# Cross attentions: where ScalarE copies the turned rows in its step

## The chip, the cores and the metric

The kernel runs on one core of a Trainium2 chip. The metric is the device time in microseconds (us) of one execution of the whole program. The program holds an attention and a feed-forward block four times over; the change touches two of the four attentions.

## The reference

`x` has 32 sequences of 128 rows of 128 numbers, and `ctx_768` holds, for each sequence, 128 rows of 96 numbers. The program is a chain, and each line is added to `x`:

```
x = x + L0_xattn(layernorm(x), ctx)         # cross attention, 16 heads of 8, with biases and wo  <- changed
x = x + L0_ffn(layernorm(x))                # 8 experts, top 1
x = x + L1_xattn(layernorm(x), ctx)         # one head
x = x + L1_ffn(layernorm(x))                # 15 experts, top 3
x = x + L2_xattn(layernorm(x), ctx, mask)   # cross attention, 16 heads of 8, masked rows         <- changed
x = x + L2_ffn(layernorm(x))                # causal self attention, 16 heads of 8, then 8 experts
x = x + L3_xattn(layernorm(x), ctx)         # 8 heads of 64
x = x + L3_ffn(layernorm(x))                # 8 experts with capacity
```

The two changed attentions compute, per sequence, with `h` the normalised rows:

```
q = h @ Wq (+ bq);  k, v = ctx @ Wk (+ bk), ctx @ Wv (+ bv)
out = softmax(q k^T / sqrt(8)) v   per head;  out @ wo + bo in L0, out itself in L2
```

## The kernel before

`attention16(p, before, kind)` builds three of the attentions: `kind` is `cross` for L0, `masked` for L2 and `self` (`causal`) for the attention inside L2_ffn. An item is one sequence, 32 in all. Each engine runs a loop of steps, `for item in unrolled(...)`, and in step t it works on several items at different depths: `item(lag)` is item t - lag. In the two cross attentions F is 1, L is 2 and O is 6. Every engine carries out its own list strictly in the order in which it is written; between the engines there are only semaphores. So the order of the calls within a step is a hand-written schedule.

For one item the path is this (engines in brackets, lag behind the name):

- [VectorE] `stats`, `aggregate` (0) and `norm` (1) make `h`; GpSimd makes the reciprocal root between them (`rsqrt`).
- [TensorE] `pe_hT` (F) turns `h` into bank `FR` of PSUM; [ScalarE] `a_hT` (F) copies these turned rows to `hT` in SBUF; [TensorE] `pe_qkv` (F) multiplies `hT` and the context by the weights, L376 and L377, into `FR` again.
- [VectorE] `v_qkv` (F) takes q and k out (L553 in the cross, L556 and L558 in the masked attention) and v (L566 or L569). `pe_turn` (L) waits for that, turns q and k, and `v_kx` and `a_qT` copy them.
- [VectorE, GpSimd] `high` and `g_low` (F + 1) split q and k into parts of fewer bits; [TensorE] `pe_stack_k` and `pe_stack_q` (L + 1) stack them, and [ScalarE] `a_qS` (four copies, L842) and `a_kS` (L834) copy the stacks to SBUF.
- [TensorE] `pe_scores` (L), in two halves, gives the scores of which `v_max` (L667) takes the maxima of each half; `pe_scoresT` (L + 2), in two halves, gives the turned scores, and [ScalarE] `a_exp` (L865) takes their exponentials, half 0 and half 1, each 128x1024.
- [TensorE] `pe_values` (L + 3) multiplies the exponentials by v and by ones, [VectorE] `v_heads` (L + 3) takes the reciprocal and multiplies (L675, L679), [TensorE] `pe_out` (O) writes the projection (or a turn back) into the bank of the k stack, and `v_residual` adds it to `X`.

The waits of the copy that the change moves, and of the two instructions that it is moved past, are these:

```
def a_hT:  wait s_qkv (an item RING earlier);  wait s_hps (it.n + 1);  copy hT <- FR;  inc s_hT
def a_kS:  wait s_st (two halves of an older item);  wait s_tk (it.n + 1);  copy kS <- TP[1];  inc s_kS
def a_exp: wait s_av (an older item);  wait s_st (2 * it.n + half + 1);  P <- exp(ST_ps);  inc s_exp
```

Who waits for them: `pe_qkv` for `s_hT`; `pe_out` (and, a step later, the turned scores and the next k stack) for `s_kS`; `pe_scoresT` of half 1 for the first half's `s_exp`, and `pe_values` for both halves.

Of the kernel before, what the change touches and what calls it, by code (L numbers as in the profile page):

```python
# [54 lines left out]
def due(value):  # L55

    return not isinstance(value, int) or value > 0
# [7 lines left out]
def unrolled(last):  # L65

    def tick(t):
        return lambda lag: Item((t - lag) // RING, (t - lag) % RING) if 0 <= t - lag < B else None
    for t in range(B + last):
        yield tick(t)  # L70


def build(nc, a, out):
    ctx = ExitStack()
    with ctx:
# [226 lines left out]
        def attention16(p, before, kind):  # L302
# [7 lines left out]
            F = 2 if causal else 1  # L310
            L = 4 if causal else 2
# [337 lines left out]
            def high(e, it):  # L649
                if due(it.n - RING + 1):  # L650
                    e.wait_ge(s_tq, at(s_tq, it.n - RING + 1))
                e.wait_ge(s_qkf, at(s_qkf, (2 if causal else 1) * (it.n + 1)))
                src = qk[:, it.s % 2].rearrange("p a h d -> p (a h) d").unsqueeze(2).broadcast_to([T, 2 * H16, 3, DH])
                dst = parts[:, it.s, :, :, 0:3, :].rearrange("p a h c d -> p (a h) c d")
                (e.copy if causal else e.tensor_copy)(dst, src).then_inc(s_hi, 1)  # L655
# [164 lines left out]
            def a_kx(e, it):  # L820
                e.wait_ge(s_turn, at(s_turn, it.n + 1))
                for j in range(4):
                    m = e.activation(kx[:, it.s % 2, j, :], FR[:, T:2 * T], ACT.Copy, scale=jmask[:, j:j + 1])
                m.then_inc(s_kx, 1)

            def a_qT(e, it):
                e.wait_ge(s_kx, at(s_kx, it.n + 1))
                e.copy(qT[:, it.s, :], FR[:, 0:T]).then_inc(s_qT, 1)

            def a_kS(e, it):  # L830
                if due(2 * (it.n - 1)):
                    e.wait_ge(s_st, at(s_st, 2 * (it.n - 1)))
                e.wait_ge(s_tk, at(s_tk, it.n + 1))
                e.copy(kS[:, it.s % 2].rearrange("p g t -> p (g t)"), TP[1]).then_inc(s_kS, 1)  # L834

            def a_qS(e, it):
                if due(2 * (it.n - 1)):
                    e.wait_ge(s_st, at(s_st, 2 * (it.n - 1)))
                e.wait_ge(s_tq, at(s_tq, it.n + 1))
                for j in range(4):  # L840
                    r = slice(32 * j, 32 * j + 32)
                    m = e.copy(qS[r, it.s % 2, :, j, :], TP[0][r, :].rearrange("p (g t) -> p g t", g=4))  # L842
                m.then_inc(s_qS, 1)

            def a_hT(e, it):
                if due(it.n - RING + 1):
                    e.wait_ge(s_qkv, at(s_qkv, it.n - RING + 1))
                e.wait_ge(s_hps, at(s_hps, it.n + 1))
                if causal:
                    e.activation(hT[:, it.s, :], FR[:, 0:T], ACT.Identity, scale=w[p + "ln"][:, 0:1]).then_inc(s_hT, 1)  # L850
                else:
                    e.copy(hT[:, it.s, :], FR[:, 0:T]).then_inc(s_hT, 1)

            def a_gate(e, it):
                if due(it.n):
                    e.wait_ge(s_gt, at(s_gt, it.n))
                e.wait_ge(s_gate, at(s_gate, it.n + 1))
                e.activation(eg[:, it.s % 3, :], TP[1][:, 0:T], ACT.Tanh, bias=half_bgate[:, 0:1], scale=0.5)\
                 .then_inc(s_eg, 1)

            def a_exp(e, it, half):
                if due(it.n - 1):
                    e.wait_ge(s_av, at(s_av, it.n - 1))
                e.wait_ge(s_st, at(s_st, 2 * it.n + half + 1))
                e.activation(P[:, it.s % 2, 8 * half:8 * half + 8, :].rearrange("p h t -> p (h t)"),  # L865
                             ST_ps[:, :, :].rearrange("p j n -> p (j n)"), ACT.Exp,
                             scale=float(DH) ** -0.5).then_inc(s_exp, 1)

            def scalar(e):
                before(e)  # L870
                e.wait_ge(s_pad, at(s_pad, n_pad))
                if causal:
                    for item in unrolled(G):
                        if it := item(L):
                            a_kx(e, it)
                            a_qT(e, it)
                        if it := item(L + 1):
                            a_kS(e, it)
                        if it := item(F + 2):
                            high(e, it)  # L880
                        if it := item(L + 2):
                            a_exp(e, it, 0)
                        if it := item(L + 1):
                            a_qS(e, it)
                        if it := item(F):
                            a_hT(e, it)
                        if it := item(G):
                            a_gate(e, it)
                        if it := item(L + 2):
                            a_exp(e, it, 1)  # L890
                else:
                    for item in unrolled(L + 3):
                        if it := item(L):
                            a_qT(e, it)
                        if it := item(L + 1):
                            a_qS(e, it)
                            a_kS(e, it)
                        if it := item(L + 2):
                            a_exp(e, it, 0)
                        if it := item(F):  # L900
                            a_hT(e, it)
                        if it := item(L + 2):
                            a_exp(e, it, 1)
            totals(stats=B, rstd=B, h=B, bn=B, ve=B, hps=B, hT=B, qkv=B, qkf=B * (2 if causal else 1), v=B,
# [7 lines left out]
            else:  # L912
                totals(**{f"ctx{i}": 16 * GROUPS for i in range(RING)})
            return dict(ahead=ahead, sync=sync, tensor=tensor, vector=vector, gpsimd=pool, scalar=scalar,
                        done=(s_done, reached["done"]))

# [1697 lines left out]
```

## Time and profile before

| | us |
|---|---|
| median of 3 runs | 2060.94 |
| lowest and highest | 2058.76 and 2067.56 |
| the profiled execution | 2070.73 |
| its span (first to last instruction) | 2068.9 |
| L0 cross attention, full steps | about 54 to 269 |
| L2 masked attention, full steps | about 873 to 1092 |

Over the span TensorE's matmuls are busy 78%, its weight loads 62%, VectorE 65%, ScalarE 46% and GpSimd 38%. In the rows below a line such as "L852" is line 852 of the kernel; PE is TensorE, PEld its weight loads, DVE is VectorE, ACT is ScalarE and POOL is GpSimd. What stands in square brackets behind a row of the timeline is the time for which the engine had been idle before it, and what ended that.

### The profile page before, as it was taken

How to read it: one execution, taken by the hardware profiler on the slowest of the kernel's cores; microseconds unless marked ns; L12 is line 12 of the kernel's file. 1: busy time of each engine (PE TensorE's matmuls, PEld its weight loads, DVE VectorE, ACT ScalarE, POOL GpSimd, SP SyncE). 2: the span in 40 equal slices, each digit the busy share in tenths (PEclk: the TensorE clock that was granted, in tenths of full speed). 3: DMA queues.
4: the chain of work that ended last, by engine and by line, in shares of the span. 5: the costliest groups of instructions: out<-in, count | busy, mean ns of one | idle time of the engine just before them, and what ended most of it. 6: DMA issues, size and time to landing. Idle time of an engine off the chain costs nothing. (4 is left out here: it accounts for less than half of the span.)

```text
span 2068.9 us, 42298 instructions
## 1 busy us (share of the span) xinstructions
PE 1615.1 (78%) x14686; PEld 1274.7 (62%) x14686; DVE 1346.9 (65%) x4040; ACT 944.5 (46%) x1817; POOL 776.0 (38%) x1156
## 2 busy tenths in 40 slices
PE   5888863877799989788885899998549799999440
PEld 3666552876677778455553566665448699997330
DVE  4777754238787777577774788886547477774632
ACT  2666630533343334366663677777124344443010
POOL 2222226345300000111213677774454544442435
PEclk9999985887799999699997799999659799999565
DMA  6132301841000000000000000000037000000043
GB/s 181 49 129 69 107 6 37 253 142 40 25 1 2 0 1 1 6 9 7 8 5 1 1 2 2 2 2 2 16 116 231 21 14 14 15 14 3 21 135 89
DMA packets 60416, 91.88 MB, mean 44 GB/s; under 512 B 11587, under 2 KB 49492, under 8 KB 59668
## 3 DMA queue, kind: packets, MB, share of 16 engines
q1 hardware_dynamic: 54068, 76.67, 12.0%
q0 software_dynamic: 6144, 12.60, 2.0%
q8 instruction: 115, 1.88, 0.4%
q14 instruction: 89, 0.73, 0.1%
HBM read 72.71 MB, written 35.39 MB: 52 GB/s over the span
## 5 line engine op out<-in xcount | busy, mean ns | idle before, releaser
L667 DVE TENSOR_REDUCE parts<-PS 128x8 fp32r<-128x1024 f32 x192 | 234.6, 1222 | 153.8 <-PE PS L424 153.6
L865 ACT ACTIVATE P<-PS 128x1024 f32<-128x1024 f32 x192 | 197.0, 1026 | 154.9 <-PE PS L439 154.7
L842 ACT CAST qS<-PS 32x512 fp32r<-32x512 f32 x384 | 220.9, 575 | 9.1 <-PE PS L391 5.7
L272 POOL TENSOR_TENSOR ve<-mv,eps_t 128x1 f32<-128x1 f32 x160 | 33.3, 208 | 444.9 <-DVE mv L268 444.9
L1636 DVE SCALAR_TENSOR_TENSOR X<-PS,wt,X 128x128 f32 (+1 forms) x480 | 134.7, 343 | 48.9 <-PE PS L1479 41.4
L1479 PEld LDWEIGHTS PS<-w_f_w,P 128*128 128x128 f32 x1024 | 131.1, 194 | 39.3 <-issue 27.2
L1768 ACT ACTIVATE P<-PS,w_f_b 128x512 f32<-128x512 f32 x128 | 88.0, 687 | 143.7 <-PE PS L1460 142.3
L1479 PE MATMUL PS<-w_f_w,P 128*128 128x128 f32 x1024 | 143.1, 284 | 13.0 <-DVE X L1636 11.2
L439 PE MATMUL PS<-qS,kS 128*128 128x512 f32 x384 | 148.9, 442 | 1.0 <-ACT P L865 1.0
L762 POOL TENSOR_TENSOR rrs<-rsq,neg_half 128x20 f32<-128x20 f32 x32 | 114.3, 3571 | 74.5 <-DVE rsq L597 74.5
L391 PE MATMUL PS<-ident_r,parts 128*128 128x128 f32 x768 | 122.0, 292 | 23.1 <-issue 22.4
L391 PEld LDWEIGHTS PS<-ident_r,parts 128*128 128x128 f32 x768 | 103.5, 201 | 37.6 <-issue 35.9
L2277 POOL DMA_INDIRECT hs<-hD,idx x96 | 93.6, 975 | 67.0 <-issue 23.8
L456 PE MATMUL PS<-P,vx 128*32 128x128 f32 x3072 | 108.7, 284 | 5.6 <-ACT P L865 5.6
L675 DVE RECIPROCAL rec<-PS 128x128 f32<-128x128 f32 x96 | 89.8, 935 | 35.0 <-PE PS L456 35.0
L456 PE MATMUL PS<-P,ones_x 128*32 128x128 f32 x3072 | 103.8, 276 | 0.0
L424 PE MATMUL PS<-kx,qT 32*128 32x512 f32 x384 | 100.9, 521 | 0.1
L274 POOL TENSOR_TENSOR rstd<-ve,neg_half 128x1 f32<-128x1 f32 x160 | 88.9, 556 | 12.5
L456 PEld LDWEIGHTS PS<-P,vx 128*32 128x32 f32 x3072 | 81.4, 113 | 18.6 <-ACT P L865 7.6
L456 PEld LDWEIGHTS PS<-P,ones_x 128*32 128x32 f32 x3072 | 78.4, 110 | 23.4 <-issue 23.4
L743 POOL TENSOR_TENSOR parts<-qk,parts 128x128 fp32r<-128x128 f32 x192 | 83.4, 454 | 20.3 <-DVE parts L655 16.7
L1296 POOL TENSOR_TENSOR parts<-ident,mx 128x1024 fp32r<-128x1024 f32 x32 | 60.8, 1899 | 63.5 <-DVE mx L1243 63.5
(299 smaller groups left out, 4243.4 us busy)
## 6 DMA issues: line engine op xcount, KB each, us to landing
tok<-hs SPq DMA_DIRECT2D x62, 128.0 KB, 3.4
hs<-yo SPq DMA_DIRECT2D x62, 128.0 KB, 3.6
P<-in_f_blob SPq DMA_DIRECT2D x12, 578.0 KB, 4.9
Y<-in_f_blob SPq DMA_DIRECT2D x11, 578.0 KB, 5.3
ctxT<-in_ctxT SPq DMA_DIRECT2D x128, 48.0 KB, 1.7
P<-in_f_blob SPq DMA_DIRECT2D x12, 450.0 KB, 4.6
Y<-in_f_blob SPq DMA_DIRECT2D x11, 450.0 KB, 4.4
w_f_w<-in_f_w SPq DMA_DIRECT2D x2, 1024.0 KB, 5.7
```

Source lines behind the costliest of these rows:

```text
L391: m = e.matmul(TP[which][:, g * T:(g + 1) * T], parts[:, it.s, which, 4 * g:4 * g + 4, :, :].rearrange("p h c d -> p (h c d)"), ident_r[:, ...
L424: m = e.matmul(S_ps[:, i, :], qT[r:r + 32, it.s, :], kx[r:r + 32, it.s % 2, :, :].rearrange("p j t -> p (j t)"), start=not causal, stop=True)
L439: m = e.matmul(ST_ps[:, i, :], kS[:, it.s % 2, g, :], qS[:, it.s % 2, g, :, :].rearrange("p j t -> p (j t)"), start=not causal, stop=True)
L456: m = e.matmul(OB[32 * g:32 * g + 32, what * T:(what + 1) * T], lhs, P[:, it.s % 2, 4 * g + j, :], start=(j == 0), stop=(j == 3))
L667: e.tensor_reduce(parts[:, it.s, 0, 8 * half:8 * half + 8, 3, 0], S_ps[:, :, :].rearrange("p i (j t) -> p (i j) t", t=T), AXX, ALU.max)\
L675: e.reciprocal(rec[:, :], OB[:, T:2 * T]).then_inc(s_rec, 1)
L762: e.tensor_tensor(rrs[:, :], rsq[:, :], neg_half[:, 0:n_heads], ALU.pow).then_inc(s_rs3, 1)
L842: m = e.copy(qS[r, it.s % 2, :, j, :], TP[0][r, :].rearrange("p (g t) -> p g t", g=4))
L865: e.activation(P[:, it.s % 2, 8 * half:8 * half + 8, :].rearrange("p h t -> p (h t)"), ST_ps[:, :, :].rearrange("p j n -> p (j n)"), ACT.E ...
L1479: m = e.matmul(YP[(n_steps * b + x) % 2][:, s * T:(s + 1) * T], lhs, w2[:, x, t * D:(t + 1) * D], start=(t == 0), stop=(t == tiles - 1))
L1636: m = e.scalar_tensor_tensor(out=X_s, in0=rows, scalar=wt[:, b, s, x:x + 1], in1=X_s, op0=ALU.mult, op1=ALU.add)
L2277: e.indirect_dma_start(hs, bass.IndirectOffsetOnAxis(ap=idx[:, i:i + 1], axis=0), hD[:, g % HR, s, :], None).then_inc(s_scat[g % HR], 16)
```

## The change

In ScalarE's list for the two cross attentions, `a_hT` stood between the two exponentials of a step. It now stands right behind `a_qS`, ahead of `a_kS` and of the first exponential. Nothing is added, removed or resized; the causal attention's list is untouched, and so is every other engine's.

```diff
@@ -894,11 +894,12 @@
                             a_qT(e, it)
                         if it := item(L + 1):
                             a_qS(e, it)
+                        if it := item(F):
+                            a_hT(e, it)
+                        if it := item(L + 1):
                             a_kS(e, it)
                         if it := item(L + 2):
                             a_exp(e, it, 0)
-                        if it := item(F):
-                            a_hT(e, it)
                         if it := item(L + 2):
                             a_exp(e, it, 1)
```

ScalarE's list in steps 3 and 4 of the L0 attention, before (qT, qS, kS and hT are the copies, P the exponentials; step 4 has the form of every later full step):

```order
L828 CAST qT<-PS 128x128
L842 CAST qS<-PS 32x4x128 x4
L834 CAST kS<-PS 128x512
L852 COPY hT<-PS 128x128
L828 CAST qT<-PS 128x128
L842 CAST qS<-PS 32x4x128 x4
L834 CAST kS<-PS 128x512
L865 ACTIVATE P<-PS 128x1024
L852 COPY hT<-PS 128x128
L865 ACTIVATE P<-PS 128x1024
```

The same two steps of ScalarE's list after the change:

```order
L828 CAST qT<-PS 128x128
L842 CAST qS<-PS 32x4x128 x4
L852 COPY hT<-PS 128x128
L834 CAST kS<-PS 128x512
L828 CAST qT<-PS 128x128
L842 CAST qS<-PS 32x4x128 x4
L852 COPY hT<-PS 128x128
L834 CAST kS<-PS 128x512
L865 ACTIVATE P<-PS 128x1024 x2
```

In step 3 the copy to hT has gone past one instruction, in step 4 and in all later ones past two, and the two exponentials now follow each other. TensorE's list, of which one full step of the L0 attention stands here, is the same before and after; L376 is the instruction that reads hT:

```order
L391 MATMUL PS<-ident_r,parts 128x128 x8
L456 MATMUL PS<-P,vx 32x128 x16
L368 MATMUL PS<-ident,h 128x128
L439 MATMUL PS<-qS,kS 128x512 x2
L424 MATMUL PS<-kx,qT 128x512 x2
L456 MATMUL PS<-P,ones_x 32x128 x16
L376 MATMUL PS<-w_a_wq,hT 128x128
L377 MATMUL PS<-w_a_wkv,ctxT 128x256
L480 MATMUL PS<-w_a_wo,oT 128x128
L424 MATMUL PS<-kx,qT 128x512 x2
L439 MATMUL PS<-qS,kS 128x512 x2
L385 MATMUL PS<-ident,qk 128x128 x2
```

Nothing has moved in it: between the turning of h (L368) and L376 there stand 20 matmuls of other items, and behind L377 come the projection, the second half of the scores, and the second half of the turned scores.

## Rows read from the trace of the kernel before

**Rows 1.** A stretch of L0: length, busy PE, PEld, DVE, ACT, POOL, granted clock, DMA, GB/s.

```profile
49.00:269.00 220.00, 185.62 (x2454) 133.75 (x2454) 163.68 (x330) 143.04 (x248) 54.95 (x138) 1.00 0.24 84
```

**Rows 2.** Waits from 49 to 269: total us, times, longest.

```profile
PE PS L376 <- ACT hT L852: 26.9, 27, 1.0
DVE qk L553 <- PE PS L377: 10.9, 26, 0.5
```

**Rows 3.** Waits from 870 to 1092.

```profile
PE PS L376 <- ACT hT L852: 27.0, 27, 1.0
...
DVE qk L556 <- PE PS L377: 11.0, 26, 0.5
```

**Rows 4.** Timeline of one full L0 step: start, us, engine, line, operation, count.

```profile
156.27 1.22 DVE L667 TENSOR_REDUCE parts<-PS 128x8 fp32r<-128x1024 f32 x1
...
157.59 0.64 PE L391 MATMUL PS<-ident_r,parts 128*128 128x128 f32 x4 [0.26 <-issue]
...
158.32 2.34 ACT L842 CAST qS<-PS 32x512 fp32r<-32x512 f32 x4
...
159.17 0.33 PE L368 MATMUL PS<-ident,h 128*128 128x128 f32 x1
...
160.32 1.08 PE L456 MATMUL PS<-P,ones_x 128*32 128x128 f32 x32
...
160.50 1.23 DVE L667 TENSOR_REDUCE parts<-PS 128x8 fp32r<-128x1024 f32 x1 [1.50 <-PE PS L424]
160.68 0.58 ACT L834 CAST kS<-PS 128x512 fp32r<-128x512 f32 x1
161.16 1.03 ACT L865 ACTIVATE P<-PS 128x1024 f32<-128x1024 f32 x1
...
162.08 0.27 ACT L852 COPY hT<-PS 128x128 f32<-128x128 f32 x1
...
162.41 0.49 PE L376 MATMUL PS<-w_a_wq,hT 128*128 128x128 f32 x2 [1.00 <-ACT hT L852]
...
162.73 0.60 PE L377 MATMUL PS<-w_a_wkv,ctxT 96*128 96x256 f32 x2
162.76 0.29 DVE L679 TENSOR_TENSOR oT<-PS,rec 128x128 f32<-128x128 f32 x1
...
163.09 0.87 POOL L743 TENSOR_TENSOR parts<-qk,parts 128x128 fp32r<-128x128 f32 x2
...
163.46 0.42 DVE L553 TENSOR_TENSOR qk<-PS,w_a_bqk 128x256 f32<-128x256 f32 x1 [0.41 <-PE PS L377]
...
163.91 0.73 PE L439 MATMUL PS<-qS,kS 128*128 128x512 f32 x2
...
164.20 1.22 DVE L667 TENSOR_REDUCE parts<-PS 128x8 fp32r<-128x1024 f32 x1
```

**Rows 5.** Timeline of L0's steps 4 and 5, which lead up to the full ones.

```profile
39.38 0.58 ACT L834 CAST kS<-PS 128x512 fp32r<-128x512 f32 x1
...
40.78 0.27 ACT L852 COPY hT<-PS 128x128 f32<-128x128 f32 x1
...
42.89 0.42 DVE L553 TENSOR_TENSOR qk<-PS,w_a_bqk 128x256 f32<-128x256 f32 x1 [2.12 <-PE PS L377]
...
43.52 1.23 DVE L667 TENSOR_REDUCE parts<-PS 128x8 fp32r<-128x1024 f32 x1
...
52.50 0.29 DVE L679 TENSOR_TENSOR oT<-PS,rec 128x128 f32<-128x128 f32 x1
52.71 0.41 DVE L553 TENSOR_TENSOR qk<-PS,w_a_bqk 128x256 f32<-128x256 f32 x1
...
53.24 1.21 DVE L667 TENSOR_REDUCE parts<-PS 128x8 fp32r<-128x1024 f32 x1
...
57.47 1.23 DVE L667 TENSOR_REDUCE parts<-PS 128x8 fp32r<-128x1024 f32 x1 [1.50 <-PE PS L424]
```

**Rows 6.** Groups of instructions from 837 to 870, L2's steps 1 to 4.

```profile
L556 DVE TENSOR_SCALAR qk<-PS,keep 128x128 f32<-128x128 f32 x4 | 1.4, 350 | 7.4 <-PE PS L377 7.4
```

## The prediction

> **What bounds the kernel now.** I read the stretches first. In the 220 us of L0's full steps VectorE is busy 163.7 us and TensorE 185.6, and the granted clock of TensorE is 1.00, the higher of its two levels (2.4 GHz) [rows 1]. No engine is full, DMA is low, so the steps are bound by a chain that goes from engine to engine. Then I read the waits. In each full step TensorE stands still once for 1.0 us, at L376, until ScalarE has written hT; VectorE stands still for 0.42 us, at the copy of q and k, until TensorE's L377 is through [rows 2, 3]. The two are one stall handed on.
>
> The timeline of one step shows how [rows 4]. From one second-half maximum (L667) to the next it is 164.20 - 156.27 = 7.93 us. TensorE has turned the rows of h by 159.17 + 0.33 = 159.50. ScalarE is then in its four copies of qS, until 160.66, and goes on to kS and the first exponential; hT comes only at 162.08 and is there at 162.35. TensorE has finished the sums of ones (L456) at 161.40 and can't go on: L376 begins at 162.41. L377 ends at 163.33, and VectorE, free since it wrote oT at 162.76 + 0.29 = 163.05, begins L553 at 163.46. Behind it v, the residual and the next maximum follow without a gap, and that maximum leads to the next step. So the rows waited 2.58 us for ScalarE, 1.0 us of it is seen on TensorE, and 0.41 us of that on VectorE, whose chain closes the loop.
>
> The loop of VectorE has one other wait, 1.50 us ahead of the first-half maximum (L667 at 160.50), for the scores [rows 4]. It hangs on h, which VectorE writes behind the previous maximum, and not on hT: it moves with the loop.
>
> **The change, step by step.** One copy of 0.27 us moves past one of 0.58 us and an exponential of 1.03 us. It issues no DMA, and no other queue changes.
>
> *What comes earlier.* hT starts where kS did, 160.68, and not at 162.08: 1.40 us earlier, ready at 160.95. L376 followed hT's start by 162.41 - 162.08 = 0.33 us, so hT would allow it at 161.01, but TensorE is in L456 until 161.40. It then begins about there, 1.0 us earlier, with no wait for hT left. L377 ends 1.0 us earlier as well, at about 162.33, and VectorE, which followed its end by 0.13 us, could have q and k at 162.46. But it is in the reciprocal and in oT until 163.05. So VectorE's own work is what is late next, and of the 1.0 us only what VectorE waited can be cashed.
>
> *How much that is.* The wait is 0.41 us from the end of oT to the start of L553. Two instructions without a wait between them overlap a little, and step 5 of L0 shows this very pair without the wait: oT at 52.50, L553 at 52.71, 0.21 us apart [rows 5], against 163.46 - 162.76 = 0.70 in the full step [rows 4]. That is a gain of 0.49 us a step. L2 has the same wait and the same oT ahead of it [rows 3], so I take 0.49 there too. The bounds are 0.42 (only the wait as booked) and 0.56 (waits of 0.5 us, the longest, and the overlap).
>
> *What comes later.* hT now stands ahead of kS and of the first exponential and delays them by its 0.27 us less the overlap of neighbours (hT began 0.11 before the exponential ended), about 0.2; bounds 0.16 and 0.27. kS then ends at 161.46. Its reader in this step is the projection behind L377, which is due near 162.1. The exponential ends at 162.39; the second half of the turned scores (L439), which needs it, is at 163.91 and 1.0 us earlier is due at 162.91. Both have 0.5 us to spare, so I cost the delay at nothing; if that cover were gone it would hold TensorE by 0.2 us a step, and the first thing to notice would be the turning of q and k, and the stacks. The second exponential follows L439 and comes with it, earlier.
>
> *Does the rest of the loop follow?* Step 5 of L0 already runs in the new form, because TensorE was late there: no wait for hT, oT and L553 back to back. Its maximum at 53.24 is followed by the next first-half maximum at 57.47, 4.23 us later [rows 5]. In the full step it is 160.50 - 156.27 = 4.23 too [rows 4]. Nothing behind the shorter tail was late. GpSimd's low parts (L743, 163.09 to 163.96) keep their distance to the first-half maximum, and now end 0.25 us behind the next maximum's start (163.71) and not before it. The k stack waits for them and would begin near 164.0 to 164.1; it is four matmuls, like the q stack's four at 157.59, which take 0.64 us [rows 4], and is through by 164.8. The q stack waits for that maximum's end at 164.9 anyway.
>
> *How many steps.* The copies of L0 run in steps 1 to 32, and those of L2 too. Steps 6 to 32 are full ones: 27 in each attention, which is the count of L376's waits [rows 2, 3]. 27 x 0.49 = 13.2 us each, 26.5 together.
>
> *The ramps.* In steps 1 and 2 nothing stands between qT and hT. In step 3 hT moves past kS alone, which is 0.48 us (start to start, as 160.68 to 161.16). In step 4 it moves from 40.78 to 39.38, 1.40 us, there is no reciprocal in VectorE's way, and VectorE waits 2.12 us for L377 [rows 5]: the whole 1.4 comes off. In step 5 TensorE is late by itself, so 0. That is 1.9 us for L0, and as much for L2, whose four copies of the ramp wait 7.4 us [rows 6]. Bounds for both: 0 and 3.8.
>
> The sum is 26.5 + 3.8 = 30.3 us. The profiled execution took 2070.7 us, with a span of 2068.9, and would take 2040.4. It lies 9.8 us above the median of the runs shown, so the median should be 2060.9 - 30.3 = 2030.6.
>
> **The clock.** The row shows 1.00 in the full steps with a gap of 1.0 us in each [rows 1, 2]. The Trainium skill, "TensorE: Matmul & The Clock Gate", A second HAM failure mode: psum-queue depth-cycling, says that short idle spells between groups of matmuls can make the clock swing between its levels. By that rule the new gaps, smaller but more of them (ahead of the turning, of the stacks), would matter, and the sum would not hold; what that would cost is worked out as a rival below. No row here shows the clock falling for gaps of this size.
>
> **The rivals.**
> 1. *VectorE's wait goes, and nothing takes its place.* As above: 2030.6, own range 2024 to 2038 (the bounds of a step, 0.42 to 0.56 times 54, give 22.7 to 30.2, with the ramps 22.7 to 34.0; 4 us for the median of few runs). Chance 0.83.
> 2. *Another wait takes part of it.* The k stack behind the low parts, or the turning of q and k behind v, comes last on TensorE and pushes the q stack and with it the scores. For it: these two waits get tighter by 0.49 us. Against: step 5 [rows 5]. Half the step gain left: 30.3 - 13.2 = 17.1, so 2044. Chance 0.09.
> 3. *The change does nothing for the end.* VectorE would then have to wait 0.49 us longer for the first-half scores, that is, TensorE, not VectorE, would be what closes the loop. For it: TensorE is busy 84% in the stretch. Against: after the maximum TensorE waits for VectorE's h, and lost 1.0 us in each step without any other engine to blame. 27 steps at no gain leave only the ramps, 3.8: 2057, within 0.5%. Chance 0.04.
> 4. *Slower: TensorE falls to its lower level.* In step 4 to 5 of L0 TensorE still ran at half rate, and from maximum to maximum it took 53.24 - 43.52 = 9.72 us [rows 5], 2.28 more than the 7.44 forecast. If the new spread of gaps put more than 30.3 / 2.28 = 13 of the 54 full steps there, the change would lose; all 54 would give 2060.9 - 30.3 + 54 x 2.28 = 2154. For it: nothing in these rows. Against: TensorE has less idle time in each step than before. Chance 0.03, and 0.01 for other harm.
>
> **How the numbers follow.** The likeliest case gives 2030.6. The range 2023 to 2042 holds case 1 nearly whole and a part of case 2. A measurement of this kernel tells about 0.5%, 10 us, from no change. Faster by more than that: cases 1 and nearly all of 2, 0.92. Within it: 0.05, case 3 and the rest. Slower: 0.03, case 4.
>
> **What would show it.** In the profile after: from maximum to maximum 7.44 us in L0's full steps; the waits L376 on hT and L553 or L556 on L377 gone; L852 1.4 us ahead of its old place against L842; the booked 1.50 us ahead of the first-half maximum unchanged; L385 newly waiting 0.1 to 0.3 us for v (L566, L569); the stretch of L0 13 us shorter, L2's too, and the feed-forward stretches unchanged. Wrong would be: 1.50 grown towards 2.0 (case 3), L391 waiting for L743 with the q stack late (case 2), a clock below 1.00 in the full steps (case 4), or L439 waiting for the exponential, which would mean that I took the cover for the moved 0.2 us too lightly.

## The result, and the profile after

The changed kernel takes 2044.96 us (median of 6 runs, 2040.32 to 2048.62) against 2062.91 before (6 runs). The ratio is 0.9903, with a 95% interval from 0.9889 to 0.9916: faster by 1.0%, 18 to 20 us. The forecast was 2030.6, with a range from 2023 to 2042. The direction was right, and the gain is some 60 to 65% of the 30.3 us forecast. Two runs of the kernel before (3044.81 and 3042.99 us) and one of fill_q below (5005.39), each far slower than all others of its kernel, are left out of every time and ratio in this document.

The profiled execution of the changed kernel took 2044.9 us, span 2043.1. Its timeline in L0, where [rows 4] showed the step before, looks like this:

```profile
147.49 1.22 DVE L667 TENSOR_REDUCE parts<-PS 128x8 fp32r<-128x1024 f32 x1
...
151.54 1.08 PE L456 MATMUL PS<-P,ones_x 128*32 128x128 f32 x32
151.72 1.23 DVE L667 TENSOR_REDUCE parts<-PS 128x8 fp32r<-128x1024 f32 x1 [1.50 <-PE PS L424]
151.90 0.27 ACT L852 COPY hT<-PS 128x128 f32<-128x128 f32 x1
152.06 0.59 ACT L834 CAST kS<-PS 128x512 fp32r<-128x512 f32 x1
152.54 1.04 ACT L865 ACTIVATE P<-PS 128x1024 f32<-128x1024 f32 x1
...
152.55 0.49 PE L376 MATMUL PS<-w_a_wq,hT 128*128 128x128 f32 x2
...
153.97 0.29 DVE L679 TENSOR_TENSOR oT<-PS,rec 128x128 f32<-128x128 f32 x1
...
154.05 0.73 PE L439 MATMUL PS<-qS,kS 128*128 128x512 f32 x2
154.18 0.41 DVE L553 TENSOR_TENSOR qk<-PS,w_a_bqk 128x256 f32<-128x256 f32 x1
...
154.85 0.44 PE L385 MATMUL PS<-ident,qk 128*128 128x128 f32 x2
...
154.91 1.22 DVE L667 TENSOR_REDUCE parts<-PS 128x8 fp32r<-128x1024 f32 x1
...
155.25 0.66 PE L391 MATMUL PS<-ident_r,parts 128*128 128x128 f32 x4
...
156.79 1.08 PE L456 MATMUL PS<-P,vx 128*32 128x128 f32 x32
```

From second-half maximum to second-half maximum it is 154.91 - 147.49 = 7.42 us; 7.44 was forecast. hT stands ahead of kS, L376 follows L456 without a wait, oT and L553 are 0.21 us apart, and the wait of 1.50 us ahead of the first-half maximum is as it was. The waits from 49 to 256 us say the same. They are total us, times, longest:

```profile
DVE parts L667 <- PE PS L424: 45.7, 28, 3.5
...
PEld PS L385 <- DVE vx L566: 14.0, 28, 0.8
...
DVE qk L553 <- issue: 0.2, 1, 0.2
```

The wait of L376 on hT and that of L553 on L377 [rows 2] are gone. So where is the rest? The two stretches of full steps, with the columns of [rows 1], name it:

```profile
47.00:259.00 212.00, 201.03 (x2529) 136.44 (x2528) 163.88 (x333) 147.60 (x255) 56.24 (x140) 0.99 0.25 87
848.00:1069.00 221.00, 198.59 (x2450) 133.38 (x2438) 165.05 (x359) 144.83 (x250) 44.41 (x112) 0.95 0.03 7
```

The granted clock was 1.00 in both before, in L0 by [rows 1] and in L2 by this row:

```profile
870.00:1092.00 222.00, 180.98 (x2419) 126.11 (x2410) 167.20 (x359) 141.76 (x246) 43.19 (x110) 1.00 0.03 7
```

Now it is 0.99 in L0 and 0.95 in L2. This is one place in L2, on TensorE and VectorE:

```profile
857.02 0.73 PE L439 MATMUL PS<-qS,kS 128*128 128x512 f32 x2
...
857.98 0.44 PE L385 MATMUL PS<-ident,qk 128*128 128x128 f32 x2 [0.23 <-DVE vx L569]
858.03 1.22 DVE L667 TENSOR_REDUCE parts<-PS 128x8 fp32r<-128x1024 f32 x1
...
858.22 0.63 PE L391 MATMUL PS<-ident_r,parts 128*128 128x128 f32 x4
...
859.35 0.63 PE L391 MATMUL PS<-ident_r,parts 128*128 128x128 f32 x4 [0.50 <-issue]
...
859.91 1.83 PE L456 MATMUL PS<-P,vx 128*32 128x128 f32 x32
...
861.81 1.20 PE L439 MATMUL PS<-qS,kS 128*128 128x512 f32 x2
...
863.79 1.23 DVE L667 TENSOR_REDUCE parts<-PS 128x8 fp32r<-128x1024 f32 x1 [3.03 <-PE PS L424]
```

The values product L456 takes 1.83 us where it takes 1.08 elsewhere, L439 takes 1.20 and not 0.72, and the first-half maximum comes 863.79 - 858.03 = 5.76 us behind the other, not 4.23. That is 1.53 us lost. The windows around it give the granted clock (the first figure behind the five engines):

```profile
857.00:859.90 2.90, 2.17 (x14) 1.54 (x12) 2.90 (x8) 1.04 (x2) 0.83 (x2) 1.00 0.06 17
859.90:863.60 3.70, 3.70 (x38) 2.27 (x37) 0.86 (x3) 3.64 (x8) 0.00 (x0) 0.54 0.01 4
863.60:868.00 4.40, 4.01 (x49) 2.68 (x47) 4.17 (x9) 1.55 (x2) 1.58 (x4) 1.00 0.04 11
```

TensorE ran at its lower level (1.2 GHz) from about 859.9 to 863.6, where the granted clock is 0.54, and then at 2.4 GHz again. I call this a fall. Such an interval of 5.76 us in place of 4.23 stands seven times in L2's 27 full steps and once in L0's; in the full steps of the profile before there is none. 8 x 1.53 = 12.2 us, and 30.3 - 12.2 = 18.1 us, against the 18.0 between the medians. (The falls are counted in one execution and the medians are over six, so a part of this close agreement is luck.)

What did TensorE do ahead of the fall? Between the turned scores (L439) and the values product (L456) its list has only the turning of q and k and the two stacks. I call this the quiet spell. In the fall above it lasts from 857.75 to 859.91, 2.16 us, with gaps of 0.23 and 0.50 us. Before the change it was, in L2:

```profile
1001.06 0.73 PE L439 MATMUL PS<-qS,kS 128*128 128x512 f32 x2
...
1001.63 0.38 PE L385 MATMUL PS<-ident,qk 128*128 128x128 f32 x2
...
1002.91 0.63 PE L391 MATMUL PS<-ident_r,parts 128*128 128x128 f32 x4 [0.50 <-issue]
1003.47 1.08 PE L456 MATMUL PS<-P,vx 128*32 128x128 f32 x32
```

That is 1.68 us, with the gap of 0.50 alone. In L0 the spell before went from 155.98 + 0.73 = 156.71 to 158.16, which is 1.45 us:

```profile
155.98 0.73 PE L439 MATMUL PS<-qS,kS 128*128 128x512 f32 x2
...
156.56 0.38 PE L385 MATMUL PS<-ident,qk 128*128 128x128 f32 x2
...
156.69 0.64 PE L391 MATMUL PS<-ident_r,parts 128*128 128x128 f32 x4
...
158.16 1.08 PE L456 MATMUL PS<-P,vx 128*32 128x128 f32 x32
```

After the change it is 156.79 - 154.78 = 2.01 us. TensorE's work between L456 and L439 moved 1.0 us earlier, but the step shortened by only 0.5. The other 0.5 of its old wait at L376 did not vanish: it came back inside the spell. In L2 most of it is a wait for v ahead of the turning, which starts 0.96 us behind the start of L439 (857.98 - 857.02) and not 0.57 (1001.63 - 1001.06). In L0 it is split. The turning starts 0.80 us behind L439's start and not 0.58, and the k stack starts 0.40 us behind the turning and not 0.13, because it now waits for GpSimd's low parts (L743).

Outside the full steps the profile before has two falls of its own, one where each attention drains (behind its last maximum). The same product in L0's drain, before and then after the change:

```profile
282.24 1.94 PE L456 MATMUL PS<-P,vx 128*32 128x128 f32 x32 [1.17 <-ACT P L865]
```

```profile
267.78 1.08 PE L456 MATMUL PS<-P,vx 128*32 128x128 f32 x32 [1.17 <-ACT P L865]
```

L2's drain shows the same, 1.93 us at 1104.82 before and 1.08 at 1079.72 after. The idle time ahead of it is 1.17 us in all four. So the same gap sometimes comes with a fall and sometimes not.

### The profile page after: what moved, and what is told of

It reads as the page before. It is cut to its first block and busy times, and to the rows that moved or that the text cites. A ratio compares the mean times of both kernels' runs of the same rounds, so it can differ in the third digit from the quotient of the medians.

```text
span 2043.1 us, 42298 instructions
## 1 busy us (share of the span) xinstructions
PE 1633.6 (80%) x14686; PEld 1274.5 (62%) x14686; DVE 1342.5 (66%) x4040; ACT 946.6 (46%) x1817; POOL 778.1 (38%) x1156
## 3 DMA queue, kind: packets, MB, share of 16 engines
q1 hardware_dynamic: 54068, 76.67, 12.2%
## 5 line engine op out<-in xcount | busy, mean ns | idle before, releaser
L439 PE MATMUL PS<-qS,kS 128*128 128x512 f32 x384 | 151.1, 449 | 1.0 <-ACT P L865 1.0
L456 PE MATMUL PS<-P,vx 128*32 128x128 f32 x3072 | 113.7, 293 | 5.6 <-ACT P L865 5.6
L456 PE MATMUL PS<-P,ones_x 128*32 128x128 f32 x3072 | 103.7, 276 | 0.0
L456 PEld LDWEIGHTS PS<-P,vx 128*32 128x32 f32 x3072 | 84.9, 116 | 19.1 <-ACT P L865 7.6
L456 PEld LDWEIGHTS PS<-P,ones_x 128*32 128x32 f32 x3072 | 78.3, 109 | 23.2 <-issue 23.1
L743 POOL TENSOR_TENSOR parts<-qk,parts 128x128 fp32r<-128x128 f32 x192 | 84.1, 458 | 20.2 <-DVE parts L655 16.5
```

Source lines behind the costliest of these rows:

```text
L439: m = e.matmul(ST_ps[:, i, :], kS[:, it.s % 2, g, :], qS[:, it.s % 2, g, :, :].rearrange("p j t -> p (j t)"), start=not causal, stop=True)
L456: m = e.matmul(OB[32 * g:32 * g + 32, what * T:(what + 1) * T], lhs, P[:, it.s % 2, 4 * g + j, :], start=(j == 0), stop=(j == 3))
```

## The experiments

**Theory A:** the falls come from that longer quiet spell. **Theory B:** they come from a TensorE that is busier in a shorter step. **Theory C:** they come by themselves, whatever the order. The number of falls below is counted from each kernel's profiled execution, as intervals from a second-half maximum to the next first-half maximum that are 1 us or more too long, behind steps 6 to 32 of L0 and L2. Each ratio is to the runs of the kernel before that were taken in the same rounds, whose median lay between 2061.4 and 2065.7 us; so compare the ratios and not the times.

| kernel | us, median | ratio to before (95%) | falls L0 + L2 |
|---|---|---|---|
| changed | 2044.96 | 0.9903 (0.9889 to 0.9916) | 1 + 7 |
| l0_only | 2048.49 | 0.9919 (0.9906 to 0.9931) | 0 + 0 |
| l2_only | 2059.10 | 0.9962 (0.9949 to 0.9975) | 0 + 7 |
| fill_both | 2030.20 | 0.9828 (0.9813 to 0.9843) | 0 + 0 |
| fill_q | 2031.26 | 0.9835 (0.9817 to 0.9852) | 0 + 0 |
| fill_turn | 2035.20 | 0.9863 (0.9843 to 0.9884) | 1 + 0 |
| before_fill | 2065.00 | 1.0015 (1.0001 to 1.0028) | 0 + 0 |
| l0_out_turn | 2043.07 | 0.9909 (0.9885 to 0.9933) | 3 + 5 |
| pad_vector | 2095.67 | 1.0145 (1.0127 to 1.0163) | 11 + 16 |
| split_turn | 2035.76 | 0.9875 (0.9851 to 0.9898) | 0 + 0 |
| split_q | 2064.33 | 1.0020 (1.0008 to 1.0032) | 0 + 0 |

**The change in one attention alone** (l0_only, l2_only; the edit is a condition on `kind` at the two places of `a_hT`).

> The copy is moved in the L0 attention alone; L2 keeps the order of before. In the profile of the changed kernel L0's full steps take 7.43 us, as forecast, with one step 1.5 us longer, and L2's take 7.55 with seven steps 1.5 us longer, in which TensorE runs at its lower level for about 3.4 us. Theory A (the shortened steps leave TensorE a longer quiet spell, turns, stacks and gaps between L439 and L456: 1.45 us before and 2.0 after in L0, 1.7 before and 2.25 after in L2): L0 gains 15.1 less one fall of 1.5, L2 has no fall and no gain: 13.6 us faster than before, 2049. Theory C (falls come by themselves, whatever the order): some falls in L2 here as well, and about 10 us of gain or less.

> The copy is moved in the L2 attention alone. Theory A: L2's steps shorten by 0.49 us (15.1 us with the ramp), and about seven of 27 lose 1.5 us to the lower clock: 4 to 5 us faster than before, 2058; L0 has no fall. Rival (the shortfall arose elsewhere, behind the attentions): L2 alone brings about 9 us, half of the 18.

L0 alone brings 0.81%, 16.7 us, about what the forecast gave for it (15.1), and has no fall, in L0 or in the untouched L2. That speaks against theory C. L2 alone brings 0.38%, 7.8 us, half of its 15.1, and has seven falls, 10.7 us. The shortfall is in L2. By time alone this run doesn't decide: the expectation was 4 to 5 us of gain and the rival's 9, and 7.8 is nearer to the rival. What decides is the trace, with its seven falls in L2. The counted execution, 2060.4 us, is also the slowest of its nine (2052.3 to 2060.4), so the others may have had fewer falls; they were not counted.

**Matmuls into the gaps** (fill_both; fill_q has the matmuls of the second edit only, fill_turn those of the first only). In all three the q stack also waits for the maximum (`s_mx`) behind its other waits and not ahead of them.

```diff
+            def pe_fill(e, it, n):
+                if due(it.n):
+                    e.wait_ge(s_qS, at(s_qS, it.n))
+                for _ in range(n):
+                    e.matmul(TP[0], ident_r[:, :], causal_q[:, :], start=True, stop=True)
...
                     for item in unrolled(O):
+                        if it := item(L + 1):
+                            pe_fill(e, it, {"masked": 1}.get(kind, 0))
                         if it := item(L):
                             pe_turn(e, it)
...
             def pe_stack_q(e, it):
                 e.wait_ge(s_lo, at(s_lo, 2 * it.n + 2))
-                e.wait_ge(s_mx, at(s_mx, 2 * it.n + 2))
                 if due(it.n):
                     e.wait_ge(s_qS, at(s_qS, it.n))
+                pe_fill(e, it, {"masked": 2, "cross": 1}.get(kind, 0))
+                e.wait_ge(s_mx, at(s_mx, 2 * it.n + 2))
```

> The changed kernel, with matmuls added whose results nobody reads (identity by a constant tile, 128x512, into the bank of the q stack ahead of that stack): in L2 one ahead of the turning of q and k and two ahead of the q stack, in L0 one ahead of the q stack. They lie in TensorE's gaps. Theory A (quiet spell): the falls go, 8 x 1.5 = 12 us faster than the changed kernel, about 2033. Theory B (the clock falls because TensorE is now busier in a shorter step): more work, so as many falls or more, 2045 or above. If the added matmuls reach past the gaps they cost up to 0.1 us a step, 5 us, on top of either.

> The changed kernel with added matmuls ahead of the q stack alone (two in L2, one in L0), none ahead of the turning. Theory A: most or all of the falls go, since the longest gap (0.50 us in L2) is filled: 2033 to 2038. Theory B: 2045 or above.

> The changed kernel with a single added matmul, in L2 alone, ahead of the turning of q and k. It halves the gap there (0.3 us) and leaves the 0.50 us ahead of the q stack. Theory A: fewer falls in L2 than seven, between 0 and 4, L0 as before with 0 to 1: 2034 to 2042. Rival (only the gap ahead of the q stack matters): seven falls, 2045.

More work on TensorE made the kernel faster: 2030.2 us, 1.7% below before, and no fall is left. Theory B is out. TensorE's list in L2 of fill_both, where L410 is the added matmul and L446 and L463 are what L439 and L456 were:

```profile
882.28 0.74 PE L446 MATMUL PS<-qS,kS 128*128 128x512 f32 x2
882.86 0.40 PE L410 MATMUL PS<-causal_q,ident_r 128*128 128x512 f32 x1
883.32 0.44 PE L385 MATMUL PS<-ident,qk 128*128 128x128 f32 x2
883.56 0.63 PE L391 MATMUL PS<-ident_r,parts 128*128 128x128 f32 x4
884.03 0.68 PE L410 MATMUL PS<-causal_q,ident_r 128*128 128x512 f32 x2
884.65 0.66 PE L391 MATMUL PS<-ident_r,parts 128*128 128x128 f32 x4
885.25 1.08 PE L463 MATMUL PS<-P,vx 128*32 128x128 f32 x32
```

From L446's end to L463 it is still 885.25 - 883.02 = 2.23 us. So it is not the spell's length by itself that counts, but that it was partly idle. Filling either gap alone is enough in L2 (fill_q leaves 0.35 us ahead of the turning, fill_turn leaves 0.55 ahead of the q stack). In fill_both and fill_q the added matmuls cost nothing: a full step takes 7.40 us in L0 and 7.53 in L2, 0.02 less than in the changed kernel. In fill_turn it takes 7.47 and 7.59, 0.05 and 0.04 more, also in L0, where nothing was added; why was not traced.

**The control: the same matmuls on the kernel before** (before_fill, the edit of fill_q).

> The kernel before, with the added matmuls ahead of the q stack (two in L2, one in L0) and nothing else: the control for what these matmuls do by themselves. Theory A (they only prevent falls of the clock, and the kernel before has none in its full steps): within 0.3% of before; a few us may come from the ramps and tails, which run partly at the lower level. Rival (they speed the kernel up in some other way, so that their gain on the changed kernel is no evidence on falls): 12 us faster here too.

No gain: 1.0015. So on the changed kernel the matmuls gained by the falls that they prevented: 8 x 1.53 = 12.2 us, and 1.1 us more from steps that are 0.02 us shorter, of the 15.5 us between the two ratios. The last 2 us are within the intervals of the ratios. The one matmul ahead of the turning in fill_both and fill_turn has no such control.

**A longer quiet spell in L0, with the same VectorE** (l0_out_turn; L0's output projection is left out, the matmul by wo is a turn back).

> The changed kernel, but L0's output projection is left out: its matmul (two passes) is replaced by a turn back, as in L2. L439 comes about 0.1 us earlier in L0's step, so TensorE's quiet spell from L439 to L456 grows from 2.0 to about 2.1 to 2.2 us, near L2's 2.25; VectorE's chain is the same. Theory A: L0 now has several falls (3 to 7, where the changed kernel has one), 3 to 9 us slower than the changed kernel. Rival (what makes L2 fall is something of its own, its period of 7.55 us or its place in the program): still one fall or none in L0, and the same time as the changed kernel.

The spell grew to 2.12 us, L0 had three falls and the changed kernel one. That is theory A's direction. But the whole had eight falls again, five of them in L2, and the time is that of the changed kernel (0.9909), not the 3 to 9 us more that were expected. With one counted execution this supports little by itself.

**A longer quiet spell in a step as long as before** (pad_vector).

```diff
                         if it := item(L):
+                            e.tensor_reduce(rsq[:, 0:1], causal_q[:, 0:400].bitcast(F32), AXX, ALU.max)
                             v_max(e, it, 1)
```

> The changed kernel, with one maximum over 400 columns of a constant tile added on VectorE (result never read) ahead of the second-half maximum of each step. It costs VectorE's chain about 0.48 us a step, so the step is back at 7.91 us in L0 and 8.03 in L2, as before the change, while TensorE's quiet spell between L439 and L456 grows to about 2.5 and 2.7 us. Theory A (the spell decides): falls in many steps, more than the changed kernel's eight in all, also in L0; slower than the kernel before by 10 us and more. Rival (it is the shorter step, a denser TensorE, that makes the clock fall): no falls, and the time of the kernel before, within 5 us.

The sharpest test. The step without a fall is 7.90 us in L0, as before the change (7.93), and TensorE has more idle time in it than the changed kernel gave it; yet there are 27 falls, 11 of them in L0 (and one more in each attention behind step 5), and the kernel is 1.45% slower than before. On TensorE, in L0, a step that did not fall, with its spell of 157.94 - 155.45 = 2.49 us:

```profile
154.72 0.73 PE L439 MATMUL PS<-qS,kS 128*128 128x512 f32 x2
155.52 0.44 PE L385 MATMUL PS<-ident,qk 128*128 128x128 f32 x2
155.91 0.66 PE L391 MATMUL PS<-ident_r,parts 128*128 128x128 f32 x4
157.37 0.64 PE L391 MATMUL PS<-ident_r,parts 128*128 128x128 f32 x4 [0.80 <-issue]
157.94 1.08 PE L456 MATMUL PS<-P,vx 128*32 128x128 f32 x32
```

```profile
50.00:268.00 218.00, 195.89 (x2236) 133.26 (x2235) 159.81 (x330) 132.14 (x226) 50.79 (x128) 0.91 0.25 84
868.00:1100.00 232.00, 200.38 (x2256) 133.63 (x2254) 165.86 (x360) 137.25 (x238) 40.87 (x104) 0.87 0.03 7
```

The second fence gives its stretches: the granted clock is 0.91 and 0.87. TensorE's list and the length of the step are those of the kernel before, and only the place of its idle time is new: no 1.0 us at L376, and 1.0 us more in the spell.

**TensorE's own work in the gaps** (split_turn, split_q: `pe_values` takes the groups (0, 1), whose exponentials are the first half's, at the early place, and (2, 3) behind the q stack).

> The changed kernel with TensorE's own work put into the gap in place of added matmuls: the half of the values product (L456 by v) that needs only the first exponential goes ahead of the turning of q and k, the other half stays behind the q stack. No instruction is added. Theory A: no falls in the full steps, 2031 to 2034, and possibly a little less. It could cost: the turning starts up to 0.5 us later, which is free while kx still waits for the maximum; and half of a product alone may run less densely.

> The same, but that half of the values product goes between the k stack and the q stack, into the gap of 0.50 us in L2 and 0.32 in L0. Theory A: no falls, 2031 to 2034. If the half takes longer than the gap, the q stack starts 0.1 to 0.3 us late, but the half behind it is shorter by as much or more, so the steps keep 7.43 and 7.55 us.

Both have no falls, but half of the values product is not half as long. In split_q, in L0:

```profile
156.55 0.66 PE L391 MATMUL PS<-ident_r,parts 128*128 128x128 f32 x4
157.15 1.07 PE L456 MATMUL PS<-P,vx 128*32 128x128 f32 x16
158.14 0.66 PE L391 MATMUL PS<-ident_r,parts 128*128 128x128 f32 x4
158.73 1.07 PE L456 MATMUL PS<-P,vx 128*32 128x128 f32 x16
```

16 matmuls take 1.07 us, and all 32 took 1.08. The halves cost a whole one more, 0.4 to 0.6 us of it on VectorE's chain, and split_q is as slow as before. I expected its steps to keep 7.43 and 7.55 us; they take 8.04 and 7.99. Split_turn has room for most of it and keeps 1.25%, 2035.8 us where 2031 to 2034 was expected.

**The changed kernel twice more** (after_again, after_third).

> The changed kernel once more, unaltered, to see how the number of falls goes with the time of an execution: 5 to 9 falls, each 1.5 us, and a time between 2040 and 2049 that is lower when there are fewer.

> The same once more: 5 to 9 falls in the full steps, most of them in L2.

They took 2039.2 us with 0 + 5 falls and 2041.4 with 0 + 6, and the profiled execution above 2044.9 with 1 + 7. So the number of falls differs from execution to execution, and in these three the time goes with it, some 1.8 to 2.2 us for each. That the falls make the whole spread of 8 us in the runs of the changed kernel is not shown: the kernel before, with no fall in its counted full steps, spreads by 9 us as well (2058.76 to 2067.56), and the slowest execution of fill_q, 2037.9 us, has none either.

## Why the prediction was wrong

*Steps that held.* The chain and what closes it; hT's 1.40 us; L376 with no wait; the 0.49 us a step (the step without a fall is 7.42 in L0, 7.55 in L2, where 7.56 follows from 8.05); the 0.2 us on kS and the exponential hidden; the ramp of L0, where L553 of step 4 came 1.96 us earlier, 0.09 of which was there before; the k stack and the turning later but without making the q stack late. With the falls prevented, fill_both measures 2030.2 us, and the forecast was 2030.6. That the two agree to 0.4 us is in part luck: as a ratio the gain is 1.7%, 35.5 us of the kernel before in those rounds (2065.7), against 30.3 forecast.

*The step that failed* is the paragraph on the clock and, from it, rival 4: the sum counts nothing for the clock. I wrote that no row showed the clock falling for gaps of this size, that nothing in the rows spoke for it, and, against it, that TensorE has less idle time in each step than before. The last is true and was the wrong question. I had noted that only 0.49 of the 1.0 us could be cashed, and even that L385 would newly wait for v, but not asked where the rest of TensorE's idle time would then lie. It moved from a place between long matmuls (ones ahead, weights behind) to one beside turns, stacks and another gap, where it cost 8 x 1.53 = 12.2 us of the 30.3. Pad_vector, in which the whole 1.0 us lies there, shows that the place alone brings the clock down, in a step of the old length.

*The size.* I treated the rival as a matter of all steps or hardly any, at 2.28 us a step, with 0.03. It came in 8 of 54 steps, at 1.53 us each: 12.2 us. A part of the falls should have been a case of its own, worked out as such; rival 2's 2044 was hit by number, but not by its mechanism: neither the low parts nor the turning made the q stack late. Case 1's own range is also too narrow by its own terms: the bounds of the gain, 22.7 to 34.0 us, and 4 us for the median give 2023 to 2042, and not 2024 to 2038; the measured 2045 lies outside both.

The rule of the Trainium skill, "TensorE: Matmul & The Clock Gate", A second HAM failure mode: psum-queue depth-cycling, was weighed and let go. The trace agrees with its outcome: short idle spells between groups of matmuls, here 0.23 and 0.50 us, and a clock that goes down and up again. By that rule the sum would not hold, and it did not. The section describes another kernel, though, and ties the idle spells to its cycling through PSUM banks. Here they are waits of the turning and the stacks for VectorE and GpSimd; no run tested the banks.

*What stays open.* Why the clock falls in some steps and not in others that look alike, and why L0, with 2.01 us against L2's 2.2, hardly falls. Between the two profiles 25.8 us lie: 22.2 in L0 and L2 together, from the first maximum to the last matmul, of which 2.7 are the two falls in the drains of the kernel before, and 3.6 in the stretches that the change does not touch. The profile before took 2070.7 us and lay 7.8 above its median, so I take these 3.6 for the spread of single executions, and did not trace it. Whether shorter added matmuls would do was not tried.

## What to carry to other kernels

When a wait on TensorE is removed and only part of it is cashed, find where the rest of the idle time comes to lie: next to turns, small stacks and other gaps it can cost more than it did beside long matmuls. Read the granted clock by stretch and look for the same product taking nearly twice its time; such falls hide in a few steps, and a mean over all steps shows them only as a clock of 0.95. The durations are the surer sign: in the kernel before, L456 took 1.94 us at 46.59, while the row of the stretch from 46 to 48 gives a clock of 1.00. Where a quiet spell can't be shortened, one or two matmuls whose result nobody reads, in the gap, are worth trying: here they turned 1.0% into 1.7%, and fill_both is the best version measured.

## What the hardware showed that I had not expected

- TensorE went to its lower level and back within about 3.7 us, in the middle of a stretch in which it was 90% busy (198.6 of 221 us), and cost 1.53 us each time.
- Added matmuls made the kernel faster by 15 us (0.9828 against 0.9903); those of them that stand ahead of the q stack (fill_q's, 0.9835) did nothing on the kernel before (1.0015).
- Half of a product that runs in four column groups takes as long as the whole: 16 matmuls 1.07 us, 32 matmuls 1.08 us, when the half has only two of the groups.
